# A two-layer attention and expert kernel: layer 1's gate in units of 6, 4 and 2 batches, and one mask operation per pair with its causal constant in PSUM

## The reference

```python
x = x + cross_attention_0(layernorm(x), ctx)       # 16 heads of 8, rotary embedding, no mask
x = x + ffn_0(layernorm(x))                        # ternary weights, width 512
# layer 1: 16 query heads on 4 key/value heads
sim = einsum('bghnd,bhsd->bghns', q, k)
mask = tril(ones(n, n))[None, None, None] & (adj != 0)[:, None, None]
attn = softmax(where(mask, sim, finfo.min))
out = layernorm(einsum(attn, v)) * ln_g + ln_b
x = x + out @ Wo.T + bo
# layer 1's feed-forward: 8 experts, each token goes to the one with the largest gate
logits = (x @ wg_red.T) @ wg_unit.T
indices, scores = argmax(softmax(logits)), max(softmax(logits))
x = x + scores * expert[indices](x)                # gelu, width 512
```

## Time and profile before

| | us |
|---|---|
| median of 3 runs (lowest, highest) | 550.77 (550.24, 551.51) |
| the profiled execution, its own time | 556.2 |
| its span, first to last instruction | 554.4 |
| busy: PE, DVE, ACT, POOL | 470.0, 402.5, 353.8, 370.7 |
| layer 1's attention and gate, from step 4 on | about 281 to 450 |
| mean granted TensorE clock, share of full speed | 0.954 |

### The profile page before, as it was taken

One profiled execution on the slowest core, in us unless ns is written; L12 is line 12 of the kernel. 1 busy time (PEld: TensorE's weight loads), 2 busy tenths in 40 slices (PEclk: granted clock), 3 DMA queues, 4 the chain that ended last, 5 costly groups with the idle time before them and its releaser, 6 DMA issues.

```text
span 554.4 us, 20049 instructions
## 1 busy us (share of the span) xinstructions
PE 470.0 (85%) x6238; PEld 365.9 (66%) x6239; DVE 402.5 (73%) x1248; ACT 353.8 (64%) x872; POOL 370.7 (67%) x755
## 2 busy tenths in 40 slices
PE   2779899999877899999899889999878607999992
PEld 2456677777655799876566556666545407999992
DVE  6697778888986687447789999999998662444441
ACT  4356688888756555663777778777666624666661
POOL 5888877878722477677667788888885551445452
PEclk9688999999989999998999999999999956999997
DMA  6664445445423910043444445555442142333330
GB/s 176 160 147 128 109 111 129 117 120 128 105 64 108 302 36 0 2 106 88 120 114 118 129 115 135 136 134 135 118 116 65 44 144 65 93 97 97 94 96 24
DMA packets 102164, 59.95 MB, mean 108 GB/s; under 512 B 20338, under 2 KB 98178, under 8 KB 102098
## 3 DMA queue, kind: packets, MB, share of 16 engines
q1 hardware_dynamic: 98738, 51.79, 37.0%
q0 software_dynamic: 2784, 6.82, 3.5%
q10 hardware_dynamic: 576, 0.53, 0.3%
HBM read 19.90 MB, written 8.81 MB: 52 GB/s over the span
## 4 chain that ended last, share of the span: by engine, by line
PE 42%; DVE 26%; issue 13%; SPq 7%; DMA 6%; POOL 3%; ACT 1%; DVEq 0%; ACTq 0%; POOLq 0%
DVE negmax L1478 10%; PE bank L699 6%; PE bank L819 5%; PE scoreT L809 5%; PE score L650 4%; DMA stack<-negpT 4%; PE bank L558 3%; SPq L483 3%; PE bank L888 3%; DVE mask L1470 2%; PE scoreT L677 2%; PE bank L589 2%; DMA stack<-pieces 2%; PE scoreT L876 2%; SPq L493 2%
## 5 line engine op out<-in xcount | busy, mean ns | idle before, releaser
L1478 DVE TENSOR_REDUCE negmax<-score 128x8 f32<-128x1024 f32 x128 | 156.1, 1220 | 32.9 <-PE score L650 31.3
L997 ACT ACTIVATE P<-scoreT 128x1024 f32<-128x1024 f32 x128 | 131.6, 1028 | 63.9 <-PE scoreT L668 39.8
L1367 POOL DMA_INDIRECT out<-by x39 | 40.3, 1032 | 52.0 <-issue 27.8
L699 PE MATMUL bank<-P,Vc 128*32 128x128 f32 x2048 | 70.6, 279 | 1.6 <-issue 1.5
L699 PEld LDWEIGHTS bank<-P,Vc 128*32 128x32 f32 x2048 | 53.0, 111 | 15.2 <-issue 8.2
L650 PE MATMUL score<-stack 64*128 64x128 bf16 x1024 | 52.6, 224 | 7.1 <-DVE negmax L1478 4.8
L650 PEld LDWEIGHTS score<-stack 64*128 64x128 bf16 x1024 | 29.9, 96 | 38.5 <-issue 25.1
L1231 POOL TENSOR_TENSOR pieces<-rest,pieces 128x256 bf16<-128x256 f32 x63 | 42.7, 678 | 4.9
L888 PE MATMUL bank<-M,P 128*128 x312 | 44.0, 285 | 0.3 <-ACT P L1131 0.3
L1228 POOL TENSOR_TENSOR pieces<-full,pieces 128x256 bf16<-128x256 f32 x63 | 42.7, 678 | 2.2 <-ACT pieces L977 1.8
L1239 POOL TENSOR_TENSOR negp<-negmax,blank 128x16 bf16<-128x16 f32 x64 | 14.0, 219 | 44.7 <-DVE negmax L1478 42.4
(11 more groups left out here) (219 smaller groups left out, 1268.4 us busy)
## 6 DMA issues: line engine op xcount, KB each, us to landing
stack<-pieces SPq DMA_DIRECT2D x192, 128.0 KB, 2.5
ctxT<-in_ctxT SPq DMA_DIRECT2D x32, 128.0 KB, 2.4
XB<-expert_rows SPq DMA_DIRECT2D x39, 66.0 KB
XA<-expert_rows SPq DMA_DIRECT2D x39, 64.0 KB
XR<-in_x SPq DMA_DIRECT2D x4, 512.0 KB, 4.8
stack<-blank SPq DMA_DIRECT2D x32, 64.0 KB, 2.1
stack<-negpT SPq DMA_DIRECT2D x64, 32.0 KB, 1.9
M<-in_M SPq DMA_DIRECT2D x1, 2048.0 KB, 9.3
```

Of the source, the lines that this page charges most:

```text
L699: mm = nc.tensor.matmul(PVOUT[VCOL * i:VCOL * (i + 1), half * 128:(half + 1) * 128], Vc[:, k % BODY, at:at + VCOL], P32[:, 2 * p_slot(L, k ...
L997: nc.scalar.activation(P32[:, at:at + 2, :], SCORET[:], ACT.Exp, scale=SCALE).then_inc(sem("exp_done"), 1)
L1367: nc.gpsimd.indirect_dma_start(out=out, out_offset=bass.IndirectOffsetOnAxis(ap=at_, axis=0), in_=by[r][:, 0:D], in_offset=None).then_inc( ...
L1478: nc.vector.tensor_reduce(negmax[:, k % 2, :, half * HQ:(half + 1) * HQ], SCORE[:].rearrange("p r (h k) -> p r h k", h=HQ), AX.X, ALU.max, ...
```

## The change

The 16 pairs of the gate become 8 units: tiles 0 to 5, 6 to 11, 12 to 17, 18 to 21, 22 to 25, 26 to 27, 28 to 29 and 30 to 31. `choose`, `place_of`, `mean_shift`, `score`, `mean_rstd` and `ranks` run once per unit, on wider operands; the statistics of a tile (`aggregate`) stay per tile. A unit is chosen three steps after its last tile's number. The choice and the counters have one buffer instead of three, and the count of a unit is one reduction. TensorE sums ranks with m+1 products for m tiles. ScalarE spreads the exponentials and the normalised rows of a unit over several steps. GpSimd's scatters begin five steps later (tile t-13 in step t) and catch up with two a step from step 28, and three in step 32.

The mask of a pair becomes one operation on 256 columns. From step 0 on its second operand is `UPPER`, a copy of `upper` that TensorE once writes to columns 128 to 255 of bank 7. Because TensorE writes maxima and outputs to the same bank, `make_mask` now stands at the end of the even step, behind waits for `negmaxT_ready` and `outT_ready`, and the next `max_transpose` waits for `mask_made`.

```diff
+UNITS = ((0, 6), (6, 12), (12, 18), (18, 22), (22, 26), (26, 28), (28, 30), (30, 32))
+UNIT_AT = {end + 3: n for n, (_, end) in enumerate(UNITS)}
+MOST = max(end - lo for lo, end in UNITS)
...
+        UPPER = bank[7][:, 128:256]
...
@@ tensor: max_transpose
+                        if L and k % 2 == 0 and is_pair(pair(k + 2)):
+                            pe.wait_ge(sem("mask_made"), count(pair(k + 2) + 1))
+                        if L and isinstance(t, int) and t == 1:
+                            nc.tensor.matmul(UPPER, eyeb[:], upper[:], start=True, stop=True)
...
@@ tensor: ranks
+                    nc.tensor.matmul(flat, before[:], chosen[:, 0:m, :].rearrange("p t e -> p (t e)"),
+                                     start=True, stop=False, skip_group_check=True)
+                    for k in range(m - 1):
+                        nc.tensor.matmul(RANKS[:, (k + 1) * EXPERTS:m * EXPERTS].rearrange("p (t e) -> p t e", e=EXPERTS), onesh[:],
+                                         chosen[:, k:k + 1, :].broadcast_to([128, m - 1 - k, EXPERTS]),
                                          start=False, stop=False, skip_group_check=True)
...
@@ gpsimd
-                    return {B: (), B + 1: (26, 27), B + 2: (), B + 3: (28, 29), B + 4: (30, 31), B + 5: ()}.get(t, (t - 8,))
+                    late = {28: (15, 16), 29: (17, 18), 30: (19, 20), 31: (21, 22), 32: (23, 24, 25), 33: (26, 27), 35: (28, 29),
+                            37: (30, 31)}
+                    return late.get(t, (t - 13,) if t < 28 else ())
...
@@ vector: make_mask
-                    for i in range(2):
-                        ins = nc.vector.scalar_tensor_tensor(mask[:, (k + i) % BODY, :], adj[turn(k)][:, i, :], 0.0, upper[:],
-                                                             ALU.is_equal, ALU.max)
-                    ins.then_inc(sem("mask_made"), 1)
+                    above = upper[:]
+                    if t >= 0:
+                        dve.wait_ge(sem("negmaxT_ready"), t + T0 + 2)
+                        if is_batch(t - 2):
+                            dve.wait_ge(sem("outT_ready"), t + T0 - 1)
+                        above = UPPER
+                    nc.vector.scalar_tensor_tensor(mask[:, k % BODY:k % BODY + 2, :], adj[turn(k)][:], 0.0,
+                                                   above.unsqueeze(1).broadcast_to([128, 2, 128]), ALU.is_equal, ALU.max
+                                                   ).then_inc(sem("mask_made"), 1)
...
@@ vector: step1
                 def step1(t, j):
+                    now, last = UNIT_AT.get(t), UNIT_AT.get(t - 1)
                     if j % 2 == 1:
                         values(j + 3)
-                        if t > B:
-                            score((t - 7) // 2)
-                    else:
-                        place_of((t - 6) // 2)
+                    if scored_first(t) is not None:
+                        score(scored_first(t))
+                    if last is not None:
+                        place_of(last)
                     maxima(t + 2, 0, j + 2)
                     add_out(t - 3, j - 3)
+                    aggregate(t - 4)
+                    tile_stats(t - 3)
                     if j % 2 == 0:
                         base_values(j + 6)
-                        make_mask(j + 4)
-                        mean_shift((t - 6) // 2)
-                    else:
-                        choose((t - 5) // 2)
+                    if now is not None:
+                        choose(now)
+                    if last is not None:
+                        mean_shift(last)
                     maxima(t + 2, 1, j + 2)
                     denominators(t - 1)
                     norm_out(t - 1)
                     out_stats(t - 1, j - 1)
-                    tile_stats(t - 3)
-                    if j % 2 == 1:
-                        carry((t - 5) // 2)
-                        if t < B:
-                            score((t - 7) // 2)
+                    if j % 2 == 0:
+                        make_mask(t, j + 4)
+                    if scored_last(t) is not None:
+                        score(scored_last(t))
```

More of the change, by code:

```diff
@@ L327, in turn, with unit_of @@
             return k // 2 % 3
+        def unit_of(tile):
+            return next(n for n, (_, end) in enumerate(UNITS) if tile < end)
         def turns(k):
@@ L750, in out_project, with ranked_at @@
                         mm.then_inc(sem("out_projected"), 1)
[L752 to L760, removed]
+                def ranked_at(t, j):
+                    if isinstance(t, int):
+                        return UNIT_AT.get(t)
+                    return body["i"] - 1 if j == 3 else None
@@ L789, in step @@
                         if L:
-                            ranks(j - 5)
+                            ranks(t, j)
                 return step
@@ new lines, in exps_at, with normals_at @@
+                def exps_at(t):
+                    for n, (lo, end) in enumerate(UNITS):
+                        if t == end + 4:
+                            return range(lo, (lo + end) // 2 if end < 26 else end)
+                        if t == end + 5 and end < 26:
+                            return range((lo + end) // 2, end)
+                    return ()
+                def normals_at(t):
+                    late = {30: (22,), 31: (23, 24, 25), 32: (26, 27), 34: (28, 29), 36: (30, 31)}
+                    if t in late:
+                        return late[t]
+                    for lo, end in UNITS[:4]:
+                        first = lo + 2 * (t - end - 6)
+                        if lo <= first < end:
+                            return (first, first + 1)
+                    return ()
@@ L1568, in carry @@
-                def carry(u):
-                    if not is_pair(u):
-                        return
-                    r = u % TURNS
-                    dve.wait_ge(sem("chosen_ready"), u + 1)
-                    nc.vector.tensor_tensor(both[:], chosen[:, r, 0, :], chosen[:, r, 1, :], ALU.add).then_inc(sem("summed"), 1)
-                    dve.wait_ge(sem("summed"), 2 * u + 1)
-                    nc.vector.tensor_tensor(sums[:, (u + 1) % TURNS, :], sums[:, r, :], both[:], ALU.add).then_inc(sem("summed"), 1)
@@ L1605, in step0, with scored_first, scored_last @@
+                def scored_first(t):
+                    return UNIT_AT.get(t - 2) if t > 30 else None
+                def scored_last(t):
+                    return UNIT_AT.get(t - 3) if t <= 28 else None
                 def step0(t, j):
```

204 lines of the change are left out of this document (107 added, 97 removed).

## The result

The changed kernel takes 594.1 us (median of 4 runs, 593.3 to 596.9) against 551.0 for the one before: 1.079 times as long, 95% interval 1.076 to 1.083, or 43 us more. The forecast was 561.9 and its range ended at 574. The direction and the place were right, the size was not.

The account below looks back on a forecast made before the run. VectorE was taken to bound the kernel, and after the change the loop through the late mask and SyncE's stack DMAs: +9.4 there and +1.7 in the tail, +11.1 on 550.77, gives 561.9 us, range 550.5 to 574.

Parts of the forecast that it names:

- VectorE's work: Layer 1, us 283 to 440: gate 17 us less, mask 9 less, together 26 of 142; busy share about 70%.
- S: The start of TensorE's even step, from which the forecast adds up the path to the next even step.
- The loop: Mask, swap and stack DMAs to TensorE's next even step: 12.30 us a pair, 13 times, 159.9 against 150.5, +9.4.
- S to the second maxima: 3.55: First term of the loop: start of TensorE's even step to that step's second maxima on VectorE, 3.55 us.
- rival A: Layer 1's loop: the mask's hand-over is hidden and lighter VectorE pays; 10.5 us a pair, 545.7 in all; chance 0.12.
- from the first stack issue to TensorE: End of the loop: fourth stack DMA begins 2.00 us after the first, lands 2.59 later, then 0.13 to TensorE.
- The tail: From step 28: GpSimd's piled-up scatters delay the last maxima split by 1.0 us and the last orstd; +1.7.
- The profiled execution's excess: Whole kernel: the median lies 5.4 us below the profiled execution, carried over unchanged, from 567.3 to 561.9.
- B: SyncE's queue stalls in every pair, as at the last one: pace 13.4 us, time 575.7; chance 0.06.
- B's sign: On SyncE, the fourth stack issue begins more than 2.2 us behind the first.
- C: VectorE's mask does not get faster, 1.33 us: pace 13.2, time 573.6; chance 0.05.
- D: Gain and loss cancel, as issues are shorter outside a profiled execution: pace near 11.5, time 551; chance 0.05.

Follow-up runs that it names:

- the filler: The changed kernel with eight unread 512-column products on TensorE while it waits for the stack before an even step: 584.5 us, 1.059 times the kernel before.
- units_one_mask_early: The changed kernel with its one mask operation reading upper from SBUF, at the old place between the even step's maxima: 553.5 us, 1.002 times the kernel before.

## Why the prediction was wrong

**VectorE's work: right in size, without effect.** The mask takes 0.42 (0.475 taken) and starts at S + 6.02 where the clock is full (6.39 less 0.475 is 5.92). VectorE's share fell to 65% (70 expected).

**The loop: the mechanism right, the pace too short.** All even steps waited for the stack, and mask, swap and stack stand as in the forecast. From the start of step 2 (268.22) to that of step 28 (453.96) the 13 loops take 185.7 us, and I had 159.9. The term that failed is the first, "S to the second maxima: 3.55". In the three loops that kept the full clock up to there it was 3.54, in the others 4.85 to 6.18: 63.0 in all, not 46.2, 16.9 too little. I had taken it from a row at full clock and did not ask what waits of about 2 us (12.3 a pair less the 10.5 of rival A), which my own sum put in front of every even step, would do to it. The rest, from those maxima to the next start, was 9.44 a pair and not 8.75: +0.15 to the mask, -0.05 for it, +0.06 for the swap's issue, and +0.5 from the first stack issue to TensorE, as landings took 2.4 to 4.1 and the four issues took 3.6 to 3.9 in three pairs. That is 9.0 over 13 loops. With the filler the way from S to the second maxima was 48.6 in all, 14.4 less, and the rest 122.0 against 122.7: what the clock cost was this term.

**The tail: too small.** Forecast +1.7, measured 46.4 against 39.8, +6.6. The last split was not 1.0 but 2.4 later behind step 28 (466.98 - 453.96 = 13.0 against 10.6): two scatters stood before it, and the maxima themselves came late. In step 32 the scatters waited 2.8 for ScalarE's normalised rows, and `orstd` came 28.7 behind step 28 where it had been 22.8. GpSimd's timeline after:

```profile
466.98 0.23 POOL L1284 TENSOR_TENSOR negp<-negmax,blank 128x16 bf16<-128x16 f32 x1
...
479.17 0.96 POOL L1333 DMA_INDIRECT expert_rows<-XR,sloti  x1 [2.82 <-ACT XR L1075]
480.43 0.96 POOL L1333 DMA_INDIRECT expert_rows<-XR,sloti  x1 [0.31 <-issue]
481.69 0.96 POOL L1333 DMA_INDIRECT expert_rows<-XR,sloti  x1 [0.30 <-issue]
482.67 0.21 POOL L1296 TENSOR_TENSOR orstd<-omv,powers 128x2 f32<-128x2 f32 x1
```

The order of the queue was read rightly; that its entries also wait for work which the units put off was not priced. How the 6.6 divide among the scatters, the late stack and the lower clock of step 28 stays open: with the scatters moved the tail was 48.2.

**The profiled execution's excess: does not carry over.** I took 5.4 us off for the difference between profile and median. Before, the profiled execution took 556.2 and the median 551.0; after, 594.6 and 594.1. So 5.4 were taken off where 0.5 were due, which is 4.9 of the error of 32.2. In the twelve experiments the profiled execution lies between 3.6 below and 3.7 above its median: the 5.4 look like that one execution's own and not like a cost of being profiled.

The sum closes on the spans: 592.8 - 554.4 = 38.4 = -1.6 (step 2 starts earlier) + 35.2 (13 loops, 185.7 against 150.5) + 6.6 (tail) - 1.9 (experts), against my +11.1. The difference of 27.3 is 16.9 and 9.0 in the loop and 4.9 in the tail, less 3.5 in the first start and the experts; with the 4.9 above it makes the 32.2.

**The rivals.** A (hidden, 10.5 a pair) is false here, but it is what the kernel does once the queue is put right: 10.86. B's sign, a fourth issue more than 2.2 behind the first, occurred in 2 of 13 pairs (2.9 and 3.1). C and D are false. That VectorE bounds the kernel before was only half right: with 0.6 us less in the mask its loop stayed at 11.44, and by the rows it was then held by GpSimd's `XR`.

## What to carry to other kernels

Before a producer is moved later, list the queue of every engine that waits for it, and ask of each entry behind that wait whether it needs the thing waited for: here four transfers did not, and moving the swap behind them was worth 43 us. When a sum puts waits like these, 1.6 us or more in every pair, in front of TensorE, price its next products at both levels of its clock.

## What the runs showed of the hardware

- A wait of about 2 us in front of TensorE can cost twice: in 10 of 13 loops the work up to the second maxima, at 1.2 GHz for all or part of it, took 4.85 us and more, against 3.54 in the other three, and filling the waits with products that nobody reads took 15.0 us out of 13 loops.
- A VectorE operation with two inputs in SBUF and a GpSimd operation beside it that reads SBUF hold each other up, and the one that starts second is stretched. The Trainium skill has this as a rule (SBUF — State Buffer, § Who interferes with whom); the trace agrees. Where GpSimd's ran already, `mshift` went from 0.15 to 0.71 us and the 256-column mask from 0.42 to as much as 0.93. Where the mask began first (345.28 in units_one_mask_early), it took 0.42 and GpSimd's cut 0.87 instead of 0.67. Making one VectorE operation shorter passed the stretch on to the next. At the late place GpSimd's `orstd` begins 0.14 behind the mask from SBUF, and 0.05 behind the one with an input in PSUM. The mask takes 0.42 both times, and `orstd`, from SBUF and from PSUM:

```profile
L1292 POOL TENSOR_TENSOR orstd<-omv,powers x11: 196/333/335, 289.1 to 430.6; 128x2 f32<-128x2 f32 x11
```

```profile
L1296 POOL TENSOR_TENSOR orstd<-omv,powers x11: 194/195/198, 290.5 to 432.2; 128x2 f32<-128x2 f32 x11
```

  So the constant in PSUM does not shorten the mask, but spares GpSimd 0.14 us; no run has it at the early place.
- The chain of waits named a GpSimd operation as releaser of a DMA that did not depend on it, in 10 of 13 pairs. A releaser is inferred, and the semaphore's count in the code has the last word.
